# A four-layer graph network on one core: adjacency turned a quarter at a time, layer 1 rows turned one block nearer to use, three of them by DMA, and the bias add of layer 0 moved

## What is computed

```python
# layer 0: graph convolution
deg = sum(adj.T, axis=1); y = deg**-0.5 * adj.T * deg**-0.5 @ (h @ W0) + bias
# layer 1: hypergraph step
head = (adj > 0) / sqrt(count of adj > 0 in the row)
inc = adj + head; y = (inc @ h) / inc.sum(-1)
# layer 2: attention with 4 heads, averaged over the heads
ht = h @ W2; e = leaky_relu(src_i + dst_j) + adj; y = softmax(e) @ ht
# layer 3: binary layer
y = relu(adj @ (max(sign(h), 0) @ sign(W3).T))
```

## Time and profile before

| what | us |
|---|---|
| median of 3 runs | 764.24 (764.19 to 768.5) |
| the profiled execution's own time | 766.52 |
| span of the profiled execution | 764.7 |
| PE busy in the span | 697.5 (91%) |
| DVE busy | 632.3 (83%) |
| ACT busy | 480.7 (63%) |
| POOL busy | 112.5 (15%) |
| DMA, mean over the span | 209 GB/s |

### The profile page before, as it was taken

One profiled execution on the slowest core, in us unless ns is written; L12 is line 12 of the kernel. 1 busy time (PEld: TensorE's weight loads), 2 busy tenths in 40 slices (PEclk: granted clock), 3 DMA queues, 4 the chain that ended last, 5 costly groups with the idle time before them and its releaser, 6 DMA issues.

```text
span 764.7 us, 16125 instructions
## 1 busy us (share of the span) xinstructions
PE 697.5 (91%) x6480; PEld 587.6 (77%) x6480; DVE 632.3 (83%) x1165; ACT 480.7 (63%) x830; POOL 112.5 (15%) x146
## 2 busy tenths in 40 slices
PE   3988999959999999999990399999999999999998
PEld 3665888848889874488880388887888888888887
DVE  6997687788998737899980499997999999998683
ACT  4996333667887227975540487657686786776751
POOL 4432121311123210011212100211000000000000
PEclk9997999988999999999995699999999999999999
DMA  9886999497879768689999994999411612026591
GB/s 329 304 291 222 426 423 292 173 221 206 183 243 247 163 169 219 173 171 268 254 245 280 313 206 111 206 255 282 167 30 29 193 56 56 4 81 194 203 395 64
DMA packets 146457, 159.54 MB, mean 209 GB/s; under 512 B 90896, under 2 KB 103888, under 8 KB 141904
## 3 DMA queue, kind: packets, MB, share of 16 engines
q1 hardware_dynamic: 127328, 117.10, 51.6%
q0 software_dynamic: 19056, 41.42, 23.6%
HBM read 76.15 MB, written 52.46 MB: 168 GB/s over the span
## 4 chain that ended last, share of the span: by engine, by line
PE 52%; DMA 16%; DVE 15%; ACT 7%; issue 4%; SPq 3%; POOL 2%; ACTq 0%; POOLq 0%; DVEq 0%
DMA adj_t<-arena 8%; PE ps L829 8%; PE ps L831 8%; PE ps L830 8%; PE ps L769 5%; DMA arena<-adj_t 4%; PE ps L871 3%; PE ps L872 3%; DVE arena L1488 3%; DVE arena L1495 3%; DMA arena<-adj_parts 3%; SPq L383 2%; DVE arena L1260 2%; PE ps L717 2%; PE ps L719 2%
## 5 line engine op out<-in xcount | busy, mean ns | idle before, releaser
L829 PE MATMUL ps<-arena 128*128 128x257 f16 x1024 | 280.6, 274 | 32.5 <-DVE arena L1495 32.2
L831 PE MATMUL ps<-arena 128*128 128x257 f16 x1024 | 280.1, 274 | 0.0
L830 PE MATMUL ps<-arena 128*128 128x257 f16 x1024 | 280.0, 273 | 0.0
L1174 ACT ACTIVATE arena<-arena 128x512 f16<-128x512 f32 x252 | 158.2, 628 | 93.5 <-PE ps L831 62.4
L1495 DVE TENSOR_TENSOR arena<-arena 128x512 f16<-128x512 f32 x256 | 175.9, 688 | 40.4 <-ACT arena L1174 40.1
L1488 DVE SCALAR_TENSOR_TENSOR arena<-arena,w_j 128x512 f32<-128x512 f32 x256 | 190.3, 744 | 0.0
L829 PEld LDWEIGHTS ps<-arena 128*128 128x128 f16 x1024 | 100.2, 98 | 47.0 <-ACT arena L1174 33.4
L830 PEld LDWEIGHTS ps<-arena 128*128 128x128 f16 x1024 | 100.5, 98 | 12.7
L831 PEld LDWEIGHTS ps<-arena 128*128 128x128 f16 x1024 | 100.1, 98 | 13.2
L717 PE MATMUL ps<-arena 128*128 128x257 f16 x256 | 71.1, 278 | 3.6 <-DVE arena L1312 3.6
L719 PE MATMUL ps<-arena 128*128 128x257 f16 x256 | 70.5, 275 | 0.0
(11 more groups left out here) (155 smaller groups left out, 1115.6 us busy)
## 6 DMA issues: line engine op xcount, KB each, us to landing
adj_t<-arena POOLq DMA_DIRECT2D x32, 1024.0 KB, 8.3
arena<-in_adj_dram SPq DMA_DIRECT2D x32, 512.0 KB, 6.0
arena<-in_adj_dram SPq DMA_DIRECT2D x16, 1024.0 KB, 5.2
adj_parts<-arena SPq DMA_DIRECT2D x16, 1024.0 KB, 25.8
arena<-adj_t SPq DMA_DIRECT2D x64, 256.0 KB, 6.1
arena<-adj_t SPq DMA_DIRECT2D x16, 1024.0 KB, 7.1
x<-arena POOLq DMA_DIRECT2D x15, 512.0 KB, 6.2
arena<-u_rows SPq DMA_DIRECT2D x4, 1024.0 KB, 14.2
```

The lines of the kernel that those rows point to most:

```text
L829: mm(ps[:, bank, 0:DE], hi, ht_hi[:, head, j, 0:DE], start=s, stop=False)
L830: mm(ps[:, bank, 0:DE], hi, ht_lo[:, head, j, 0:DE], start=False, stop=False)
L831: ins = mm(ps[:, bank, 0:DE], lo, ht_hi[:, head, j, 0:DE], start=False, stop=e)
L1174: nc.scalar.activation(p_hi[:, j % 4, :], prob[:, j % 4, :], copy).then_inc(p_hi_done, 1)
```

## The change

- **Quarters.** SP turns four pieces (the next quarter's), then calls `load_e` for that quarter, and only then goes on to the pieces after. `WIDEN_AFTER` is spread to match: piece 6 after group 0, 7 after 1, 8 after 3, 9 and 10 after 4, 11 after 5, 12 after 7, 13 and 14 after 8, 15 after 9. The two early loads for layer 3 come after the last `load_e`.
- **Layer 1 nearer.** PE turns row t+3 in row t instead of t+4; sign and count are of row t+5 instead of t+6, the fill of row t+4 instead of t+5. Row 5's count leaves the layer 0 stage (`COUNTS` has five entries). Rows 0 and 1 are multiplied together: groups 0 to 2 of both, then group 3 of both.
- **Three rows by DMA.** Rows 9, 12 and 15 are not turned by PE; ACT and DVE split them in natural order and SP turns them by DMA, from one buffer.
- **Bias.** Its buffer moves to where `hrelu` was, so SP loads it after the adjacency and two rows, and POOL adds it after the degree roots. DVE waits for each block's add; ACT no longer waits.

Further places where only an index is renamed for `PE_ROWS` are left out of the diff.

```diff
--- before.py
+++ after.py
@@ -130,8 +130,8 @@
         w3_s = view(G0 + 6 * KB, [DC, D], F16)
-        b0_bc = view(G0 + 7 * KB, [D], F32)
         hrelu = view(160 * KB, [2, D], F32)
+        b0_bc = view(160 * KB, [D], F32)
@@ -148,6 +148,7 @@
         inc_nat = [view(off, [2, N], F16) for off in (24 * KB, 48 * KB)]
+        inc_nat_l1 = view(64 * KB, [2, N], F16)
@@ -186,12 +187,14 @@
-        COUNTS = (1, 2, 9, 10, 11, 14)
+        COUNTS = (1, 2, 9, 10, 11)
...
         AHEAD = 5
-        WIDEN_AFTER = {0: (6, 7), 1: (8, 9), 2: (10, 11), 4: (12, 13), 5: (14, 15)}
+        DMA_ROWS = (9, 12, 15)
+        PE_ROWS = [t for t in range(AHEAD, NB) if t not in DMA_ROWS]
+        WIDEN_AFTER = {0: (6,), 1: (7,), 3: (8,), 4: (9, 10), 5: (11,), 7: (12,), 8: (13, 14), 9: (15,)}
@@ -351,7 +354,6 @@
             sp.dma_start(w0_f, w0_d.rearrange("(c p) d -> p c d", p=P)).then_inc(w0_in, 16)
-            sp.dma_start(b0_bc, b0_d.partition_broadcast(P)).then_inc(bias_in, 16)
@@ -369,9 +371,12 @@
             def turn_inc(t):
-                sp.wait_ge(inc_lo_done, t + 1)
+                sp.wait_ge(inc_lo_done, t + 1 if t < AHEAD else AHEAD + 1 + DMA_ROWS.index(t))
+                if t >= AHEAD:
+                    sp.wait_ge(l1_ps, t - AHEAD + 1)
+                natural = inc_nat[t % 2] if t < AHEAD else inc_nat_l1
                 for part in range(2):
-                    sp.dma_start_transpose(out=inc_parts[t % AHEAD][:, part, :, :], in_=inc_nat[t % 2][:, part, :]
+                    sp.dma_start_transpose(out=inc_parts[t % AHEAD][:, part, :, :], in_=natural[:, part, :]
@@ -387,6 +392,8 @@
                 load_rows(t)
+            sp.wait_ge(h0_lo_done, NB)
+            sp.dma_start(b0_bc, b0_d.partition_broadcast(P)).then_inc(bias_in, 16)
@@ -419,10 +426,15 @@
                 turn_adj(n)
-            for t in range(12, NB):
+            for t in range(12, 14):
                 reload_rows(t)
+            turn_inc(DMA_ROWS[0])
+            for t in range(14, NB):
+                reload_rows(t)
+            turn_inc(DMA_ROWS[1])
...
                 turn_adj(n)
+            turn_inc(DMA_ROWS[2])
@@ -448,18 +460,12 @@
             sp.wait_ge(ht_ps, 2 * NB)
-            for n in range(QB, 3 * QB):
-                turn_adj(n)
             for q in range(1, NQ):
-                if q == 2:
-                    for n in range(3 * QB, 4 * QB):
-                        turn_adj(n)
-                if q == NQ - 1:
-                    for g in range(TG):
-                        sp.wait_ge(wide[g], 16 * NQ)
-                    for i in range(2):
-                        sp.dma_start(adjt_early[i], adjt_dram[i]).then_inc(adjt_in[4 + i], 16)
+                for g in range(TG):
+                    turn_adj(QB * q + g)
                 load_e(q)
+            for i in range(2):
+                sp.dma_start(adjt_early[i], adjt_dram[i]).then_inc(adjt_in[4 + i], 16)
@@ -503,14 +509,13 @@
                                         neg_half[:, XP * p:XP * p + XP], ALU.pow).then_inc(rstd_done, 1)
-            pool.wait_ge(bias_in, 16)
-            for t in range(NB):
-                pool.wait_ge(relu0, t + 1)
-                nc.gpsimd.tensor_tensor(x[:, t, :], x[:, t, :], b0_bc, ALU.add).then_inc(bias_added, 1)
...
                                         ).then_inc(dinv_done, 1)
+            pool.wait_ge(bias_in, 16)
+            for t in range(NB):
+                nc.gpsimd.tensor_tensor(x[:, t, :], x[:, t, :], b0_bc, ALU.add).then_inc(bias_added, 1)
@@ -554,8 +559,8 @@
                     inverse_root2(t - 1)
-                if t + 6 < NB:
-                    inverse_count(t + 6)
+                if t + 5 < NB:
+                    inverse_count(t + 5)
@@ -701,10 +706,10 @@
                 bank = ACC[t % 3]
-                if t >= AHEAD:
-                    pe.wait_ge(part_lo_done, 4 * (t - AHEAD) + g + 1)
+                if t in PE_ROWS:
+                    pe.wait_ge(part_lo_done, 4 * PE_ROWS.index(t) + g + 1)
                 elif g == 0:
-                    pe.wait_ge(inc_in[t], 32)
+                    pe.wait_ge(inc_in[t % AHEAD], 32 * (t // AHEAD + 1) if t < AHEAD else 64)
@@ -744,10 +749,14 @@
             pe.wait_ge(deg_copied, 1)
-            for t in range(NB):
+            for groups in (range(NB // TG - 1), (NB // TG - 1,)):
+                for t in range(2):
+                    for g in groups:
+                        products1(t, g)
+            for t in range(2, NB):
                 for g in range(NB // TG):
-                    if AHEAD <= t + 4 < NB:
-                        transpose_group(t + 4, g)
+                    if t + 3 in PE_ROWS:
+                        transpose_group(t + 3, g)
@@ -948,7 +957,6 @@
             act.wait_ge(hw_ps, NB)
-            act.wait_ge(bias_added, NB)
@@ -972,9 +980,14 @@
                     act.wait_ge(nat_sent[3], 48)
+                elif t < AHEAD:
+                    act.wait_ge(inc_in[t - 2], 32)
+                elif t == DMA_ROWS[0]:
+                    act.wait_ge(wa_part, 4 * HEADS)
                 else:
-                    act.wait_ge(inc_in[t - 2], 32)
-                nc.scalar.activation(inc_nat[t % 2][:, 0, :], inc[:, t % 2, :], copy, scale=ADJ_SCALE
+                    act.wait_ge(inc_in[DMA_ROWS[DMA_ROWS.index(t) - 1] % AHEAD], 64)
+                natural = inc_nat[t % 2] if t < AHEAD else inc_nat_l1
+                nc.scalar.activation(natural[:, 0, :], inc[:, t % 2, :], copy, scale=ADJ_SCALE
@@ -1022,23 +1035,25 @@
             for t in range(NB):
-                more = AHEAD <= t + 4 < NB
+                more = t + 3 in PE_ROWS
                 if more:
-                    part_high(t + 4, 0)
-                if t + 6 < NB:
-                    sign(t + 6)
+                    part_high(t + 3, 0)
+                if t + 3 in DMA_ROWS:
+                    inc_high(t + 3)
+                if t + 5 < NB:
+                    sign(t + 5)
                 if more:
-                    part_high(t + 4, 1)
+                    part_high(t + 3, 1)
...
                 if more:
-                    part_high(t + 4, 2)
+                    part_high(t + 3, 2)
...
                 if more:
-                    part_high(t + 4, 3)
-                if t + 6 < NB:
-                    count(t + 6)
+                    part_high(t + 3, 3)
+                if t + 5 < NB:
+                    count(t + 5)
@@ -1317,10 +1332,9 @@
-            dve.wait_ge(bias_added, NB)
-
...
                 b = t % 2
+                dve.wait_ge(bias_added, t + 1)
@@ -1356,13 +1370,13 @@
                     dve.wait_ge(nat_sent[1], 32)
-                if t >= AHEAD + 2:
-                    dve.wait_ge(t_ps, 4 * (t - AHEAD - 2) + 4)
+                if t - 2 in PE_ROWS:
+                    dve.wait_ge(t_ps, 4 * PE_ROWS.index(t - 2) + 4)
@@ -1370,8 +1384,9 @@
             def inc_low(t):
-                dve.wait_ge(inc_hi_done, t + 1)
-                v.scalar_tensor_tensor(inc_nat[t % 2][:, 1, :], inc[:, t % 2, :], ADJ_SCALE, inc_nat[t % 2][:, 0, :],
+                dve.wait_ge(inc_hi_done, t + 1 if t < AHEAD else AHEAD + 1 + DMA_ROWS.index(t))
+                natural = inc_nat[t % 2] if t < AHEAD else inc_nat_l1
+                v.scalar_tensor_tensor(natural[:, 1, :], inc[:, t % 2, :], ADJ_SCALE, natural[:, 0, :],
@@ -1420,22 +1435,24 @@
             for t in range(NB):
-                more = AHEAD <= t + 4 < NB
+                more = t + 3 in PE_ROWS
...
                 if more:
-                    part_low(t + 4, 0)
+                    part_low(t + 3, 0)
...
                 if more:
-                    part_low(t + 4, 1)
+                    part_low(t + 3, 1)
...
                     inc_low(4)
-                if t + 5 < NB:
-                    fill(t + 5)
+                if t + 3 in DMA_ROWS:
+                    inc_low(t + 3)
+                if AHEAD <= t + 4 < NB:
+                    fill(t + 4)
                 if more:
-                    part_low(t + 4, 2)
-                    part_low(t + 4, 3)
+                    part_low(t + 3, 2)
+                    part_low(t + 3, 3)
...
                 if 1 <= t <= 4:
```

More of the change, by code:

```diff
@@ L687, in transpose_group @@
             def transpose_group(t, g):
-                n = 4 * (t - AHEAD) + g
+                n = 4 * PE_ROWS.index(t) + g
                 if g == 0:
@@ L774, in _ @@
             pe.wait_ge(w2_lo_done, 4)
-            pe.wait_ge(part_lo_done, 4 * (NB - AHEAD))
+            pe.wait_ge(part_lo_done, 4 * len(PE_ROWS))
             pe.wait_ge(l1_taken, NB - 1)
```

## The result

The changed kernel takes **745.5 us** (median of four runs, 743.1 to 748.7) against 766.4 for the kernel before in the same comparison: ratio 0.973, 95% interval 0.967 to 0.979. It is faster, as forecast, but 730 was forecast with a range of 721 to 741, and 745.5 lies above it. The profiled execution took 743.45 us, 23.1 less than that of before, where the sum had said 34.0. (The forecast of 730 also took 2.3 us off because the profiled run stood above the median shown; over eleven runs of the kernel before in the last comparison the median is 767.4, so that step was worth nothing.)

What follows compares the result with a forecast made beforehand. PE was near its pace except for a hole before quarter 1 (ACT awaiting an adj_t load) and layer 1, partly paced by DVE. Profiled 766.5 less 34.0 gave 732.5; less 2.3 for the median, 730 us, range 721 to 741.

Steps and rivals of the forecast that it cites:

- the sum: Whole kernel: gains of 30.4 (quarters), 0.5 (front) and 3.1 (layer 1, bias delay included) make 34.0 us.
- Part 1, the quarters: Layer 2: four turns instead of eight ahead of quarter 1's load; 30.4 us gained, ends 25.3 and 36.4.
- all three passages: Layer 2: gaps between DVE's head_inverse into quarters 1, 2 and 3, forecast at 22, 24 and 24 us.
- Part 2, the bias: Layer 0: later adds make the first inverse root 6.0 us late; 3.8 (0.9 to 7.3) arrive at layer 1.
- the front: Ahead of the adjacency: one DMA less on SP and L1260 without a neighbour; 0.5 us gained, ends 0 and 2.
- Part 3, the nearer rows: Layer 1: one DVE pass less gains 8.1 us; first transposes starting later cost 3.0.
- Part 3, the DMA rows: Layer 1: rows 9, 12 and 15 each free PE of 1.8 us; half counted, 1.8 gained in all.
- The DMA rows arrive late: Rival, layer 1: row 15 lands 6 us after row 14's end and PE waits; 736 us, chance 6%.
- The two larger rivals: Bias adds cost all that layer 1 gives (20%, 735.5 us); every quarter's passage costs as quarter 2's now (14%, 735.3).

Runs made afterwards that it cites:

- the version without rows and long waits: Changed kernel with no DMA-turned rows and POOL's widening and adding for pieces 0 to 3 issued later: 727.6 us, ratio 0.950; repeat 729.3 us, 0.952.
- row 15 alone: The version without rows and long waits, with only row 15 of layer 1 turned by DMA: 727.7 us, ratio 0.950.
- row 9 alone: The version without rows and long waits, with only row 9 of layer 1 turned by DMA: 732.3 us, ratio 0.955.

## Why the prediction was wrong, step by step

**Part 1, the quarters: right.** 31.3 us gained in layer 2 against 30.4, with all three passages within 1.0 us of their forecast.

**Part 2, the bias: the mechanism right, the size wrong.** The adds began when the bias had landed, at 77.2, and ended at 90.2, as forecast. The adds as a group (durations in ns, minimum/median/maximum, first and last start) and the first root in POOL's timeline:

```profile
L518 POOL TENSOR_TENSOR x<-x,arena x16: 714/719/1705, 77.2 to 89.5; 128x256 f32<-128x256 f32 x16
...
90.22 0.55 POOL L523 TENSOR_TENSOR rstd<-var_eps,neg_half 128x1 f32<-128x1 f32 x1
```

The root is 6.0 us later than in the earlier trace rows, as forecast. Most adds came nearer to their minimum (median 719 ns) than the 0.9 us taken, and the later start (77.2, not 75.8) made up for it. But of the 6.0 only 1.4 us were left at the end of layer 0, not 3.8, and the front gained 1.8 and not 0.5: `nat` low halves took 1222 ns each, all of them (maximum 1226), where the earlier trace rows have up to 1745. The sum of part 2 was put at 3.3 lost, and is 0.4 gained by these means, which is not told from nothing. (In the two traces of before and after alone it is 0.9 lost.)

The rule of the Trainium skill that was weighed there ("SBUF — State Buffer", section "Who interferes with whom") is borne out add by add. Only two of DVE's maxima, which read two SBUF inputs, ran beside the adds. An add beside the first (from 79.3) and one beside the second took 1.7 us each, the other fourteen about 0.72; and these two maxima took 1.76 and 1.74 us where the median of all 16 is 1.22. The mistake was to read the rule as slow adds throughout, without counting which DVE operations would run beside them. The second pair, from the timelines of POOL and DVE, and all maxima:

```profile
84.46 1.71 POOL L518 TENSOR_TENSOR x<-x,arena 128x256 f32<-128x256 f32 x1
...
83.84 1.74 DVE L1332 TENSOR_TENSOR arena<-arena 128x2048 f16<-128x2048 f16 x1
...
L1332 DVE TENSOR_TENSOR arena<-arena x16: 1217/1218/1760, 78.7 to 161.5; 128x2048 f16<-128x2048 f16 x16
```

**Part 3, the nearer rows: over-valued.** The term was 8.1 (one DVE pass less) less 3.0 for the later start, so 5.1. The start is right: the first transposes of L702 run at 174.54, 3.5 us after the earlier trace rows, of which 0.9 come from layer 0 in this trace. But the length of layer 1 is 119.0 us with nearer rows and 118.1 without. With POOL's waits out of the way it is 114.8 to 115.9 against 118.2: 2.3 to 3.4 us at best. One pass less was counted as if the gain, once made, were kept. It is made: from layer 0's last take to the third row sums it is 23.2 us in the version without rows and long waits (its repeat) and 28.2 in the kernel with the quarters alone, 5.0 gained. After that 2.7 are given back. One pass takes 9.4 us instead of 7.3; there ACT's `sign` waits 2.21 us for a reloaded row of `adj` (1.32 in the first run of this version, where the pass takes 8.5, and 0.61 with the quarters alone). Near the end, where PE sets the pace, the passes from 252.79 to 265.71 take 12.9 us and their like 11.0 (255.52 to 266.55). The other passes give 1.3 back.

**Part 3, the DMA rows: the step that failed.** I wrote "Each frees PE of 1.8 us, but DVE is close behind the earlier trace rows, so I count half, 1.8 in all", and, under added waits, that "nothing else on SP waits behind it but `load_e(0)`". Both look at PE, DVE and SP's order and at nothing else: the overlap of the turns with POOL's DMAs was put at nothing. The runs showed 7.7 us lost in layer 1's length, 12.5 in the time. The date for row 15 was wrong too: its turn was to land around 266 and be wanted at about 271, but was issued at 269.27 and had landed whole at 283.6. The prediction named PE waiting for row 9, 12 or 15 as a sign of being wrong, and it came true for rows 9 and 15. The turn's 1.8 us of PE are real (row 15 alone), but rows 9 and 12 lie where DVE sets the pace and where the widening runs. The largest wait that was missed is on another queue: POOL's inverse roots stand behind its DMA waits. It could have been seen. Before the change POOL already waited 3.76 us for a widening at 241.09, and ACT 7.0 us for roots, and part 1 of the same prediction had weighed how two queues' transfers slow each other (11.7 beside 7.7) for the loads. The Trainium skill says it in "DMA: Bandwidth & Descriptors", section "Issuing engines are not separate DMA queues": transfers started by any engine run on the same 16 DMA engines and interleave. These traces agree, with the widening's DMAs at a median of 10.3 us with the turned rows and 7.7 without them. How the 7.7 us lost divide between POOL's roots, the rows' own lateness, the waits for `fill` and the clock is not shown.

The terms, though read from several traces, add up. Against the sum of 34.0: part 1 +0.9, part 2 +3.7, the nearer rows -6.0 (from 5.1 to -0.9), the DMA rows -9.5 (from 1.8 to -7.7). That makes 23.1, and the profiled executions differ by 23.1. That it fits to the tenth is chance: the terms for part 2 and the nearer rows come from other traces than these two, whose own spans differ by 31.3 in layer 2, -0.9 ahead of layer 1 and -7.1 in it, 23.3 in all.

**The rivals.** None had it. "The DMA rows arrive late" was nearest. It was given 6%, and PE does wait 3.5 us for DMA-turned rows in the changed kernel; but it priced only the turned row's own lateness. The two larger rivals did not come about: the bias costs nothing that can be told, and of the passages only the last is dearer than forecast, by 1.0 us.

## What to carry to other kernels

Work moved from a busy engine to DMA isn't free when the DMA engines are near full in that stretch. Add up the queues' shares in a window of the trace first (84% before, 113% after), as a warning and not as a rule, since one row at 103% cost nothing; then look at whose DMA gets slower and what stands behind the wait for it. An in-order queue that mixes long DMA waits with one-column operations on a critical chain hands the whole delay to that chain, so issue the wait where the DMA has surely landed. How much of the delay counts depends on the lead: with rows turned one block nearer to use, waits that were hidden before cost 3 to 4 us. Test the parts of a change one by one: here one part alone was faster than all three.

## What the runs showed of the hardware

- One half of a row (128x2048 f16) turned by DMA within SBUF lands in 4.6 us (median, 8.0 at most) with no widening beside it, and in 9.7 (13.3 at most) beside it; with row 9 alone the two halves took 11.8 and 15.6. The 1 MB DMAs of the widening go from a median of 7.7 to 10.3 us with the turned rows. The slowing is mutual.
- A GpSimd add of 128x256 takes 0.72 us, and 1.7 when a DVE maximum of two SBUF inputs runs beside it; the maximum then takes 1.74 to 1.76 us instead of 1.22. So each of the two slows the other.
- In two traces a window of 5 us in which PE was short of work (3.15 and 3.53 us busy) is followed by one at a granted clock of 0.71 or 0.66, at once or one window later, with matmuls at up to twice their time. Being short isn't enough: without the DMA rows PE was busy for 2.74 of 5 us (from 245 us), and the clock stayed at 1.00 there and in the next window. What else such a drop needs isn't shown.
